# A dense attention and mixture-of-experts kernel: when GpSimd's last indirect scatters are issued

## The reference

```python
x = x + xattn(layernorm(x), ctx, W_qkv, W_out, b_out)      # 16 heads of 64
x = x + moe(layernorm(x), Wg, bg, Wgu, bgu, Wd, bd)

# moe: 16 experts, each token goes to its 2 best
logits = xt @ Wg.T + bg
top_vals, top_idx = top_k(logits, 2);  rw = softmax(top_vals)
gate, up = split(xt @ Wgu[e] + bgu[e])
out_e = ((clip(up, -7, 7) + 1) * (min(gate, 7) * sigmoid(1.702 * gate))) @ Wd[e] + bd[e]
out = sum over the two experts of rw * out_e
```

## Time and profile before

| | us |
|---|---|
| median of three timed runs | 601.31 |
| span of the profiled execution | 636.7 |
| PE busy in it | 542.6 (85%) |
| DVE busy | 519.7 (82%) |
| ACT busy | 484.4 (76%) |
| POOL busy | 450.0 (71%) |

### The profile page before, as it was taken

How to read it: one execution, slowest core, us unless ns; L and a number is a source line. 1 busy time by engine, 2 the same in 40 slices (tenths; PEclk the granted TensorE clock), 3 DMA queues, 4 the chain that set the end, 5 groups by cost and what they waited for, 6 DMA issues and landing times.

```text
span 636.7 us, 20049 instructions
## 1 busy us (share of the span) xinstructions
PE 542.6 (85%) x6760; PEld 457.3 (72%) x6760; DVE 519.7 (82%) x1482; ACT 484.4 (76%) x1366; POOL 450.0 (71%) x555
## 2 busy tenths in 40 slices
PE   2899999999999999999999999977778687778700
PEld 1578898988999889889898899876435565556500
DVE  5879999999999999999999999988756456465516
ACT  1899999999999999999999999978425445455410
POOL 8996585988989889889898898753533455545530
PEclk9999999999999999999999999999789879898755
DMA  9772383174062947228337407550122332221139
GB/s 258 222 274 53 59 287 68 46 261 124 19 185 72 308 132 248 60 57 302 81 55 267 125 12 221 175 119 3 28 62 70 82 82 66 69 69 56 33 115 302
DMA packets 69701, 81.63 MB, mean 128 GB/s; under 512 B 8116, under 2 KB 47564, under 8 KB 69604
## 3 DMA queue, kind: packets, MB, share of 16 engines
q1 hardware_dynamic: 56244, 67.60, 36.8%
q0 software_dynamic: 4352, 8.47, 4.0%
q10 hardware_dynamic: 9008, 4.30, 2.5%
HBM read 18.82 MB, written 46.31 MB: 102 GB/s over the span
## 4 chain that ended last, share of the span: by engine, by line
PE 66%; DVE 9%; issue 7%; ACT 7%; DMA 3%; ACTq 2%; another core or an unknown queue 2%; POOL 2%; SPq 0%; POOLq 0%
PE bank L1258 15%; PE bank L1259 15%; PE bank L1260 15%; PE bank L1378 8%; PE bank L1430 5%; PE bank L1466 3%; DMA ctx_sb<-results 2%; ACT probs L564 2%; PE bank L1497 1%; PE bank L1524 1%; ACTq L462 1%; POOL results L833 1%; DVE pT L1071 1%; ACT pT L576 1%
## 5 line engine op out<-in xcount | busy, mean ns | idle before, releaser
L564 ACT ACTIVATE probs<-bank,nbias 128x128 f32<-128x128 f32 x512 | 146.4, 369 | 4.2
L833 POOL DMA_INDIRECT results<-z,stage x72 | 71.0, 986 | 73.3 <-ACT z L618 53.0
L1071 DVE TENSOR_TENSOR pT<-bank,pT 128x512 f16<-128x512 f32 x128 | 87.6, 684 | 10.9 <-ACT pT L576 7.8
L1050 DVE TENSOR_REDUCE qmax<-bank 128x4 f32<-128x512 f32 x128 | 87.1, 680 | 2.0 <-remote 1.4
L1260 PE MATMUL bank<-keys,q_pad 128*128 128x128 f16 x480 | 86.7, 219 | 0.3 <-issue 0.3
L1259 PE MATMUL bank<-keys,q_pad 128*128 128x128 f16 x480 | 86.6, 219 | 0.0
L1258 PE MATMUL bank<-keys,q_pad 128*128 128x128 f16 x480 | 86.6, 219 | 0.0
L576 ACT ACTIVATE pT<-bank 128x512 f16<-128x512 f32 x128 | 78.2, 611 | 7.2 <-PE bank L1378 4.6
L1378 PE MATMUL bank<-ident,probs 128*128 128x128 f32 x512 | 78.4, 276 | 5.5 <-DVE pT L1071 2.9
L770 POOL DMA_INDIRECT places<-payload,slots x64 | 65.3, 1020 | 16.3 <-issue 11.8
L1258 PE MATMUL bank<-xT,w_qkv 128*128 128x256 f16 x256 | 69.9, 273 | 1.1 <-DVE xT L879 0.8
(11 more groups left out here) (261 smaller groups left out, 2015.5 us busy)
## 6 DMA issues: line engine op xcount, KB each, us to landing
places<-z SPq DMA_DIRECT2D x8, 4160.0 KB
q_pad<-q_nat SPq DMA_DIRECT2D x120, 128.0 KB, 2.4
stage<-places SPq DMA_DIRECT2D x64, 65.0 KB
ctx_sb<-results SPq DMA_DIRECT2D x14, 256.0 KB, 5.0
ctx_sb<-in_ctx_dram ACTq DMA_DIRECT2D x4, 512.0 KB, 10.6
stage<-in_L_ffn_Wgu_dram SPq DMA_DIRECT2D x1, 2048.0 KB, 9.5
out_dram<-x_sb ACTq DMA_DIRECT2D x7, 256.0 KB, 5.5
stage<-in_L_xattn_W_qkv_dram SPq DMA_DIRECT2D x3, 512.0 KB, 6.6
```

The costliest lines, as they stand in the source:

```text
L564: last = nc.scalar.activation(probs[:, b, k, :], score_bank[b][:, k * P:(k + 1) * P], ACT.Exp, bias=nbias[:, b, k:k + 1], scale=exp_scale)
L833: nc.gpsimd.indirect_dma_start(out=results, out_offset=bass.IndirectOffsetOnAxis(ap=to, axis=0), in_=z[:, (q - 5) % NZ, t, :], in_offset=None,
L1050: nc.vector.tensor_reduce(qmax[:, r % 2, :], score_bank[r % 2][:, :].rearrange("p (h k) -> p h k", h=4), AX.X, ALU.max).then_inc(s["qmax_o ...
L1071: nc.vector.tensor_tensor(pT[:, r % 2, LO, :], pt_bank[:, :], pT[:, r % 2, HI, :], ALU.subtract).then_inc(s["pt_lo"], 1)
```

## The change

At p = 15 each of the four scatters of pair 12 gets a wait of its own: before the scatter in step r GpSimd waits until the scores of the same step, n = 8p + r, stand (`score_mm` at 8p + r + 1). At p = 16 the four scatters of pair 13, which stood in step 1, stand one each in steps 1 to 4, in the same order, and each waits until the outputs of n-6 are transposed (`ot_mm` at 8p + r - 5), which PE does in step r-1. Nothing else is changed; the scatters of pairs 14 and 15 stay where they are.

```diff
                     if p <= PAIRS and pair_live(p - 3):
                         if r == 0:
                             finish_rows(p - 3)
-                        if p == PAIRS and r == 1:
-                            scatter(p - 3, (0, 1))
+                        if p == PAIRS and 1 <= r < 5:
+                            wait(pool, "ot_mm", p * STEPS + r - 5)
+                            scatter(p - 3, ((r - 1) // 2,), ((r - 1) % 2,))
                         elif p < PAIRS and r in (1, 2, 4, 5):
+                            if p == PAIRS - 1:
+                                wait(pool, "score_mm", p * STEPS + r + 1)
                             scatter(p - 3, (r // 4,), ((r + 2) % 3,))
```

## The result

| | before | changed |
|---|---|---|
| median of 20 timed runs each | 601.54 us | 602.94 us |
| ratio to before | 1 | 1.0027 [1.0015, 1.0038] |
| span of the profiled execution | 636.7 us | 601.2 us |

The changed kernel is slower by 0.27%, some 1.6 us (0.9 to 2.3). The bracket behind a ratio is its 95% interval; the ratio is taken over all runs and is not the quotient of the two medians, which would be 1.0023. I had forecast 601.6 us and "within 0.2%"; 602.94 lies above the range of the forecast, and the interval of the ratio has values on both sides of 0.2%. One timed run of the study, 734.12 us at a mean granted clock of 0.733 for TensorE where every other has 0.937 or more, is in none of the ratios.

The account below looks back on a forecast made before the run. PE bounds attention to 420 us, then a chain of PE, ACT and DVE. Profiled: 636.7 - 3.7 + 0.3 = 633.3 us; timed, the gain vanishes: 601.3 + 0.3 = 601.6 us, range 597.8 to 602.6.

Parts of the forecast that it names:

- Attention up to 420 us is bound by PE, only the drain counts: From 30 to 420 us PE works 386.88 of 390 us; only p = 15 and 16, to about 456 us, matter.
- In the profiled execution a run of scatters holds back what the others hear from PE: Four-scatter runs at p = 15 and 16 cost 2.1 and 1.6 us, together 3.7, bounds 2.5 and 4.3.
- Timed runs hardly have the late waits: Late waits on PE account for almost all 35.4 us between profile and timed median; the 3.7 us gain shrinks to nothing.
- The waits at p = 15 cost nothing: Pair 12's spread scatters end near 433.5 us, with over 5 us to spare on both sides.
- The four steps at p = 16: Pair 13's scatters in steps 3 and 4 make L672 late; cost 0.1 to 0.9 us, taken as 0.3.
- GpSimd is late for the last pair: L672 over 1.2 us late behind scatters at p = 16; price 0.9 to 2, 602.2 to 603.3 us; chance 0.14.
- the late waits are real: Late waits after scatter runs occur in timed runs too: 597.9 us at full size, 600.1 at 40%; chance 0.29.
- What would show it: Spread scatters, no remote waits, L672 3 to 4 us earlier right behind a scatter, span about 633, timed median not following.

Follow-up runs that it names:

- the control: The kernel before, unchanged, timed and profiled once more on a chip of the first kind: 602.79 against 602.61 us, ratio 1.0004 [0.9993, 1.0015], span 601.2 us.
- two by two: The changed kernel with pair 13's four scatters two each in steps 1 and 2 of p = 16: 601.93 against 601.92 us, 0.9998 [0.9986, 1.0011].
- the kernel with the memset: The kernel before with an unneeded 3.53 us GpSimd memset ahead of L672: 606.0 against 601.92 us, 1.0074 [1.0052, 1.0095].
- The four kernels of the table: Against the kernel before: four steps of p = 16 alone +1.0 us, changed kernel +1.6, two scatters in step 4 +2.7, memset ahead of L672 +4.5.
- the four steps alone: The kernel before with only the p = 16 half of the change, no waits at p = 15: 604.26 us, 1.0016 [1.0001, 1.0032].
- two scatters in step 4: The kernel before with pair 13's last two scatters in step 4 of p = 16, no waits: 605.31 against 602.66 us, 1.0045 [1.0030, 1.0060].

## Why the prediction was wrong

*Attention up to 420 us is bound by PE, only the drain counts*: right, PE is busy 386.96 of 390 us in the changed kernel too.

*In the profiled execution a run of scatters holds back what the others hear from PE*: right, and shown on the fourth chip, where the late waits of p = 16 go with the run and those of p = 15 stay. I had 1.6 us for the run at p = 16; the traces differ by 2.26, of which up to 1.0 may be PE's clock. For the run at p = 15 I had 2.1; no run took that one apart on such a chip. Of my bounds, the 1.98 us in the upper one stands in none of the rows that I gave.

*Timed runs hardly have the late waits*: right for the chips on which they were timed (601.3 to 602.7 us), and it kept the 3.7 us out of the forecast. But I took it for a difference between recording and timing ("late are only waits on a PE with many instructions to record"). It is one between chips, and there a timed run gains, by 0.1 to 3.5 us.

*The waits at p = 15 cost nothing*: right as far as can be told, 1.0006 [0.9994, 1.0019]. I put the scatters near 421, 423, 429 and 432 us; they start at 419.6, 421.3, 426.8 and 428.7.

*The four steps at p = 16, "cost 0.1 to 0.9 us; I take 0.3, nearer the end that the trace shows"*: this is the step that failed. The queue is as I had described it, behind `egap` a scatter, `finish_rows`, a scatter, and the first of pair 14, then L672. The cost is 0.83 us at `y` and 1.6 us (0.9 to 2.3) in time, where the term had 0.3. Three faults are in it.

First, the two halves of the argument didn't match. I had written that the chain from `egap` to L672 would be shorter by 0.5 to 0.8 us where PE isn't held up, and that GpSimd's work doesn't shrink with it; and I had concluded that timed runs are such executions. In the control the chain from `denominators` to L672 is 451.41 - 446.63 = 4.78 us, for 5.57 in the earlier trace rows: 0.8 shorter. So the upper bound was the value to take, not 0.3. Nor was it only that PE isn't held up: PE's granted clock is 0.59 from 449 to 452 us and 0.50 from 452 to 455 us in the trace of before, and where it is full (two by two) the chain takes 4.33 us. The 0.66 us for two transpositions that I read in the earlier trace rows is also what the two of `y` take at a granted clock of 0.50, for 0.41 at 1.00.

Second, I priced L672's lateness, which is only 0.29 us, and not what L686 and L689 meet when they are late. DVE's two L1036 begin 0.03 us after L686 in the control, and 0.12 us before it in the changed kernel, where L686 takes 0.48 us more. In the kernel with the memset they begin 0.03 us before it, and it still takes 0.18 us. So the cost isn't a slope but a step, somewhere between 0.03 and 0.12 us.

Third, I let lateness of `y` count once. The four kernels of the table give 1.2 to 2.0 us of time for each us of lateness, though the intervals don't exclude 1. Why it should be more than 1 isn't shown; 0.4 us of it in the changed kernel's trace, between `y` and the last scatter, go with PE's lower clock.

*Rival "GpSimd is late for the last pair"*: this is what happened, in its place and with its price of 0.9 to 2 us (1.6 measured). That the price fits is in part luck, for it was added up from a lateness of 1.2 us and a late wait of PE, and neither came. Its point of decision was wrong: I let it begin once L672 was 1.2 us late, and held "PE does little there" against it; 0.29 us was enough, through DVE. A chance of 0.14 was too small for it, and my range ended at 602.6, inside its 602.2 to 603.3.

*Rival "the late waits are real"*: not on the chips of the timed comparison, real on the fourth.

*What would show it*: L672 behind a scatter with less than 0.1 us of idle time, held; that it came 6.2 us earlier than in the earlier trace rows, and not 3 to 4, is the other chip's doing. "A span of about 633" did not come, since the profile was taken on a chip of the other kind; L672 late "by over 1 us" was the wrong alarm.

## What to carry to other kernels

When work is moved into idle time of an in-order queue, count the idle time in an execution like those that are timed, up to the instruction that the last chain needs, and look at what each instruction behind it runs beside: a lateness of 0.3 us became 0.8 when two small GpSimd operations slid beside a VectorE instruction with two SBUF inputs. If the profiled span and the timed median are several per cent apart, run the kernel before once more ahead of all else: the profile may show another chip's waits. And a change that is worth something on one chip (0.9972 [0.9945, 0.9999], without the waits) can cost on another (1.0016 [1.0001, 1.0032], with them).

## What the runs showed of the hardware that I had not expected

- Chips differ in kind. The kernel before takes 601.9 to 602.7 us on three and 640.6 on a fourth. From 30 to 420 us the traces of both kinds agree (PE busy 386.8 to 387.0 us). Of the 35.5 us between the trace of before and the control, 5.0 lie ahead of the last scatter to `places` and 30.5 behind it. Waits of ACT and DVE are marked "remote" there, with 0.2 to 5.6 us of idle time, where GpSimd issues indirect scatters close behind each other; in the expert stage its scatters are idle 52.7 us for ACT instead of 25.0. PE's mean granted clock is 0.937 to 0.957 in the timed runs on the fourth chip and 0.964 to 0.978 in those of the same kernel on the others. Why the chips differ, the traces don't show.
- On such a chip the stretch with the scatters at p = 16 takes 17.49 us with four in a row, 16.13 and 16.34 with three, and 15.23 with single ones in steps of their own, one execution each; a part of that may be PE's clock.
- A GpSimd operation on 128x2 numbers takes 0.19 us alone and 0.67 beside a VectorE instruction with two SBUF inputs (L686), another 1.09 instead of 0.72 (L674).
- The same work can meet another clock. With 1.81 us of idle time ahead of `y` PE's granted clock was 0.84 and 0.59 in the two stretches from 450 to 462 us of one trace (the changed kernel) and 1.00 in both of another (the four steps alone); with 2.83 us of idle time (two scatters in step 4) it was 1.00 and 0.72. The lower one went with 0.5 us in the profiled chain and nothing that can be seen in timed runs.
